# A router on rows before their normalisation, and a third down piece of 64 rows, in a one-core decoder layer

## The reference

```python
x = layernorm(x + attn(x, W_Q, W_K, W_V, W_O))                 # causal, 16 heads of 128
x = layernorm(x + xattn(x, ctx, Wq, Wg, bg, Wkv, Wo))          # linear cross attention with a gate, 375 keys
logits = x @ router_weight.T + router_bias                     # 8 experts
top_vals, top_idx = top_k(logits, 2); top_w = softmax(top_vals)
gate, up = split(x @ gate_up_proj[e] + gate_up_bias[e])        # H = I = 512
act = (clip(up, -7, 7) + 1) * min(gate, 7) * sigmoid(1.702 * min(gate, 7))
expert_out = act @ down_proj[e] + down_bias[e]
x = layernorm(x + sum over the two chosen experts of top_w * expert_out)
```

## Time and profile before

| | |
|---|---|
| median of 3 runs | 853.14 us (853.09 to 853.36) |
| the profiled execution | 854.54 us, of which 852.7 us are its span |
| TensorE busy | 832.9 us, 98% of the span, 4919 products |
| VectorE, ScalarE, GpSimd busy | 479.0, 319.1 and 97.3 us |
| read and written in memory | 64.10 and 31.53 MB |
| cross attention's last product to the first expert's first | about 625 to 649.9 us |
| the eight experts | 649.9 to about 836 us |

### The profile page before, as it was taken

How to read it: one execution, slowest core, us unless ns; L and a number is a source line. 1 busy time by engine, 2 the same in 40 slices (tenths; PEclk the granted TensorE clock), 3 DMA queues, 4 the chain that set the end, 5 groups by cost and what they waited for, 6 DMA issues and landing times.

```text
span 852.7 us, 12622 instructions
## 1 busy us (share of the span) xinstructions
PE 832.9 (98%) x4919; PEld 733.2 (86%) x4919; DVE 479.0 (56%) x878; ACT 319.1 (37%) x718; POOL 97.3 (11%) x92
## 2 busy tenths in 40 slices
PE   9999999999999999999999999999988999999995
PEld 7989898989899998988899888888867888888884
DVE  4536455363736462675760254455577687777765
ACT  4543324242433432442543222212233365555434
POOL 0000000000000000000000000110231244343432
PEclk9999999999999999999999999999976999999998
DMA  9990735533020003003110101110287366665235
GB/s 321 350 309 7 232 110 174 163 99 106 26 80 7 26 7 124 3 4 136 51 37 1 33 4 37 62 62 1 89 321 214 127 204 202 193 182 168 51 59 188
DMA packets 35759, 97.39 MB, mean 114 GB/s; under 512 B 6665, under 2 KB 9225, under 8 KB 33009
## 3 DMA queue, kind: packets, MB, share of 16 engines
q1 hardware_dynamic: 32224, 88.69, 30.8%
q0 software_dynamic: 3472, 7.87, 4.5%
HBM read 64.10 MB, written 31.53 MB: 112 GB/s over the span
## 4 chain that ended last, share of the span: by engine, by line
PE 93%; DVE 3%; ACT 2%; issue 1%; DMA 1%; POOL 0%; ACTq 0%; SPq 0%; POOLq 0%; DVEq 0%
PE bank L316 74%; PE bank L701 3%; PE bank L605 3%; PE bank L735 3%; PE bank L628 2%; PE bank L796 2%; PE bank L687 1%; PE bank L984 1%; PE bank L773 1%; PE bank L814 1%; ACT prob L1140 1%; PE bank L852 1%; DVE w_gu L1433 1%; DMA xg<-x_rows 0%; DMA x_rows<-row,slot_u 0%
## 5 line engine op out<-in xcount | busy, mean ns | idle before, releaser
L316 PE MATMUL bank<-w_kv,cT 128*125 128x512 f32 x576 | 143.6, 400 | 0.0
L316 PE MATMUL bank<-xT,w_qkv 128*128 128x512 f32 (+1 forms) x672 | 137.8, 365 | 0.8 <-ACT qT L1130 0.8
L316 PEld LDWEIGHTS bank<-xT,w_qkv 128*128 128x128 f32 x672 | 122.1, 188 | 15.8 <-ACT qT L1130 1.1
L316 PEld LDWEIGHTS bank<-w_kv,cT 128*125 128x125 f32 x576 | 104.2, 186 | 23.8
L316 PE MATMUL bank<-x_g,w_gu 128*128 128x288 f32 x768 | 111.2, 303 | 3.7 <-DVE x_g L1433 2.9
L316 PEld LDWEIGHTS bank<-x_g,w_gu 128*128 128x128 f32 x768 | 107.1, 194 | 5.3 <-issue 3.2
L501 POOL TENSOR_TENSOR ln_rs<-ln_ve,half 128x1 f32<-128x1 f32 (+2 forms) x16 | 11.3, 705 | 616.5 <-DVE ln_ve L1562 603.5
L316 PE MATMUL bank<-w_o,zT 128*128 128x512 f32 x336 | 78.7, 392 | 0.0
L316 PE MATMUL bank<-w_qkv,xT 128*128 128x256 f32 x588 | 77.3, 287 | 0.0
L316 PEld LDWEIGHTS bank<-w_o,zT 128*128 128x128 f32 x336 | 62.4, 188 | 12.7
L316 PEld LDWEIGHTS bank<-w_qkv,xT 128*128 128x128 f32 x588 | 72.2, 191 | 0.0
(11 more groups left out here) (174 smaller groups left out, 1202.5 us busy)
## 6 DMA issues: line engine op xcount, KB each, us to landing
x_rows<-blank SPq DMA_DIRECT2D x9, 2084.0 KB, 16.5
raw_gu<-in_w_gu_dram SPq DMA_DIRECT2D x8, 2048.0 KB
raw_w<-in_w_qkv_dram SPq DMA_DIRECT2D x22, 512.0 KB, 9.0
raw_dn<-in_w_down_dram SPq DMA_DIRECT2D x8, 1024.0 KB, 8.9
raw_c<-in_ctx_t_dram SPq DMA_DIRECT2D x8, 750.0 KB, 4.3
raw_o<-in_w_o_dram SPq DMA_DIRECT2D x8, 512.0 KB, 4.3
xg<-x_rows SPq DMA_DIRECT2D x8, 512.0 KB, 6.2
raw_kv<-in_w_kv_dram SPq DMA_DIRECT2D x2, 1024.0 KB, 6.8
```

The costliest lines, as they stand in the source:

```text
L316: last = nc.tensor.matmul(mm_out, lhs(a, k), rhs(b, k), start=(k == 0 and i == 0), stop=(k == n - 1 and i == 2))
```

## The change

1. **Router on the added rows.** `turn_x2` transposes `acc` after `cross_add`, not `row` after the normalisation. Since the logits are linear in the row, `choose` scales them by `ln_rs` and adds `rt_c`, which is the router's bias less mean x deviation x the column sums of the router's weights. `router_sums` makes these sums once, by four products behind the gates; `x2_norm` makes `shift` and `rt_c` for each tile. At the end the order is another: `turn_x2(5)` ahead of the last pass of `cross_out(6)`, `router(6)` ahead of `rank(5)`, `choose(5)` ahead of `x2_norm(6)`, on ScalarE a weight split between the two copies.
2. **First rows by part.** The first expert's rows are read in three transfers with a semaphore each, TensorE waits for each by itself, and SP issues nothing further until all three have landed.
3. **Third down piece.** For experts 0 to 5 the 32 high and the 32 low columns of `hT` lie side by side, and `down_stacked` takes both as one operand of 64 columns against the high weights, and the 32 high ones against the low weights: 8 products for 12. Rows 32 to 63 of the result are scaled as well and added to memory by a fourth adding transfer (`add_stacked`), which waits for the first three to land and stands behind `gated(e + 2, 0)` on GpSimd. `h_low` splits in two operations.
4. **Order in the first two experts.** High and low halves of the second expert's rows ahead of `swish` and `clamp`; the split of the first `w_dn` ahead of the loop on ScalarE and in two halves in parts 1 and 2 on VectorE; the weights of the third expert split a part earlier (`SPLITS`).

```diff
-            last = [("rk", 4), ("st", 0), ("t1", 5), ("rt", 5), ("t1", 6), ("rk", 5), ("rt", 6), ("db", 0), ("rk", 6),
+            last = [("rk", 4), ("st", 0), ("t1", 5), ("rt", 5), ("t1", 6), ("rt", 6), ("rk", 5), ("db", 0), ("rk", 6),
...
-        SPLITS = {0: ((3,), (), (), (), ()), 1: ((), (), (), (0,), (1, 2, 3))}
+        SPLITS = {0: ((3,), (), (), (), ()), 1: ((), (), (0,), (1,), (2, 3))}
...
-            for e in range(3):
+            for k, (p0, rows) in enumerate(PIECES):
+                sp.dma_start(xg[0][0:rows, k, :], x_rows_of(p0, rows)[:, 0:D]).then_inc(in_first[k], 16)
+            for k in range(3):
+                sp.wait_ge(in_first[k], 16)
+            for e in range(1, 3):
                 rows_in(xg[e], e * ROWS, in_xg[e])
...
+            def add_stacked(e):
+                p0, rows = PIECES[2]
+                pool.wait_ge(add_done, added_by(e) + 48)
+                nc.gpsimd.indirect_dma_start(
+                    y_acc, bass.IndirectOffsetOnAxis(ap=meta[0:rows, 2, e, NE:NE + 1].bitcast(U32), axis=0),
+                    y[rows:2 * rows, (3 * e + 2) % 4, :], None, bounds_check=T + DUMP - 1, oob_is_err=True,
+                    compute_op=ALU.add).then_inc(add_done, 16)
+
             for e in range(NE + 1):
                 if e < NE:
                     for q in range(KC):
                         gated(e, q)
+                        if q == 0 and 0 <= e - 2 < STACKED:
+                            add_stacked(e - 2)
...
             def turn_x2(n):
-                pe.wait_ge(m["row_ok"], n + 1)
+                pe.wait_ge(*done("wo", n))
...
-                    mm = nc.tensor.transpose(o[:, k * P:(k + 1) * P], row[:, n, k * P:(k + 1) * P], ident[:, :])
+                    mm = nc.tensor.transpose(o[:, k * P:(k + 1) * P], acc[:, n, k * P:(k + 1) * P], ident[:, :])
...
+            def router_sums():
+                pe.wait_ge(m["z_lo"], 4 * NP_)
+                pe.wait_ge(in_late, 16 * 2)
+                o = take(route, "ws", 0)
+                for k in range(KC):
+                    mm = nc.tensor.matmul(o[:, 0:NE], all_ones[:, :], rt_w[:, k, :], start=(k == 0), stop=(k == KC - 1))
+                mm.then_inc(ready("ws", 0)[0], 1)
...
-            cross_out(6)
+            cross_out(6, PASSES[0:2])
             turn_x2(5)
+            cross_out(6, PASSES[2:3])
             router(5)
             turn_x2(6)
+            router(6)
             rank(5)
-            router(6)
...
+            def down_stacked(w, hid, bk):
+                p0, rows = PIECES[2]
+                for b, i in ((0, 0), (1, 0), (1, 1), (0, 1), (1, 2), (0, 2), (1, 3), (0, 3)):
+                    wide = rows if b else 2 * rows
+                    mm = nc.tensor.matmul(banks[bk][0:wide, :], hid[:, i, p0:p0 + wide], w[:, b, i, :],
+                                          start=(b == 0 and i == 0), stop=(b == 0 and i == 3))
+                mm.then_inc(m["dn_mm"], 1)
...
             for k in range(3):
                 gather_high(0, k)
+            dn_high(0, 0)
...
-                    swish(e, q)
                     if e == 0 and q:
                         gather_high(1, q - 1)
+                    swish(e, q)
...
             def x2_norm(n):
                 normalise(1, n, n + 3, row[:, n, 0:D], "row_ok")
+                s = n % 2
+                nc.vector.tensor_tensor(shift[:, s:s + 1], ln_mv[:, 1, n, 0:1], ln_rs[:, 1, n:n + 1], ALU.mult)\
+                    .then_inc(m["rtc_ok"], 1)
...
+                nc.vector.scalar_tensor_tensor(rt_c[:, s], rt_s[:, :], shift[:, s:s + 1], rt_b[:, :], ALU.mult, ALU.add)\
+                    .then_inc(m["rtc_ok"], 1)
...
+                nc.vector.scalar_tensor_tensor(logit[:, s], bank("rt", n)[:, 0:NE], ln_rs[:, 1, n:n + 1], rt_c[:, s],
+                                               ALU.mult, ALU.add).then_inc(done("rt", n)[0], 1)
...
-                split_lo(hid[:, 1, q], hh[:, q % 2], hid[:, 0, q]).then_inc(m["h_lo"], 1)
+                for p0, rows in (PIECES[2], (0, 2 * P)):
+                    lo = split_lo(hid[:, q, hidden_cols(1, p0, rows)], hh[:, q % 2, p0:p0 + rows],
+                                  hid[:, q, p0:p0 + rows])
+                lo.then_inc(m["h_lo"], 1)
...
-                    clamp(e, q, gu_b[:, e])
                     if e == 0 and q:
                         gather_low(1, q - 1)
+                    if e == 0 and q in (1, 2):
+                        dn_low_half(0, 0, q - 1)
+                    clamp(e, q, gu_b[:, e])
```

More of the change, by code:

```diff
@@ L234, in decoder_layer @@
         in_xg = [sem(f"in_xg{j}") for j in range(3)]
+        in_first = [sem(f"in_first{k}") for k in range(3)]
         in_last = [sem(f"in_last{s}") for s in range(2)]
@@ L279, in route_order @@
         def route_order():
-            steps = []
+            steps = [("ws", 0)]
             for n in range(5):
@@ L336, in decoder_layer, with hidden_cols, added_by @@
         LAST_E = NE - 1
+        STACKED = NE - 2
+        def hidden_cols(a, p0, rows):
+            first = CAP + (p0 + CAP - 2 * P) % CAP if a else p0
+            return slice(first, first + rows)
+        def added_by(e):
+            return 48 * e + 16 * min(e, STACKED)
         HELD = (P, P, 2 * (CAP - 2 * P))
@@ L920, in _ @@
                 gate(j)
+            router_sums()
             for b, chunks in enumerate(CHUNKS):
@@ L1027, in down @@
                     pe.wait_ge(m["xg_lo"], 3 * (e + 2) + 2)
-                down_piece(w_dn[e % 2], hT[e % 2], k, y_bank(e, k))
+                if k == 2 and e < STACKED:
+                    down_stacked(w_dn[e % 2], hT[e % 2], y_bank(e, k))
+                else:
+                    down_piece(w_dn[e % 2], hT[e % 2], k, y_bank(e, k))
             for k in range(6):
@@ L1349, in y_evac @@
                 if i >= 4:
-                    act.wait_ge(add_done, 48 * ((i - 4) // 3 + 1))
-                rows = PIECES[k][1]
-                scaled(e, k, y_bank(e, k), i % 4, meta[0:rows, k, e, e:e + 1])
+                    held = (i - 4) // 3
+                    act.wait_ge(add_done, added_by(held + 1) if i % 3 == 0 else added_by(held) + 48)
+                rows = PIECES[k][1] * (2 if k == 2 and e < STACKED else 1)
+                scaled(e, k, y_bank(e, k), i % 4, meta[0:rows, k, e, e:e + 1], rows)
             def gather_high(e, k):
@@ L1380, in _ @@
                     y_evac(e - 1, 1)
-                if more:
+                if e and more:
                     dn_high(e, e % 2)
@@ L1701, in dn_low, with dn_low_half @@
                 split_lo(w_dn[s][:, 1], raw_dn[s], w_dn[s][:, 0]).then_inc(m["dn_lo"], 1)
+            def dn_low_half(e, s, h):
+                if h == 0:
+                    dve.wait_ge(m["dn_hi"], e + 1)
+                part = slice(h * KC // 2, (h + 1) * KC // 2)
+                last = split_lo(w_dn[s][:, 1, part], raw_dn[s][:, part], w_dn[s][:, 0, part])
+                if h:
+                    last.then_inc(m["dn_lo"], 1)
             nc.vector.memset(idle, 1.0).then_inc(m["gate_ok"], 1)
@@ L1816, in _ @@
             split_lo(dn_b[1][0:NE, :], raw_dnb[0:NE, :], dn_b[0][0:NE, :]).then_inc(m["dnb_lo"], 1)
+            dve.wait_ge(*ready("ws", 0))
+            nc.vector.tensor_scalar(rt_s[:, :], bank("ws", 0)[:, 0:NE], -1.0, None, ALU.mult).then_inc(done("ws", 0)[0], 1)
             for b, chunks in enumerate(CHUNKS):
@@ L1870, in _ @@
             cross_stats(6)
+            choose(5)
             x2_norm(6)
-            choose(5)
             assign(5)
```

48 lines of the change are left out of this document (28 added, 20 removed).

## The result

The changed kernel takes 844.88 us (median of 4 runs, 844.43 to 846.58) against 853.25 us of the kernel before on the same chip (853.09 to 854.08). The ratio is 0.9897, 95% interval 0.9884 to 0.991: 8.4 us less, where 10.8 were forecast (842.3 us, from 839.3 to 847.8). It lies in that range and 0.4 above the narrower one, 840 to 844.5, that the main forecast had. The spans of the profiled executions, 852.7 and 843.2, differ by 9.5.

A forecast was written before the change was run, and what follows sets the result against it. TensorE, busy 98% of the span, bounds the kernel. Terms 1.0 + 0.1 - 2.1 - 1.3 - 3.0 + 0 - 5.5 = -10.8 take the profiled 854.54 to 843.7, as median 842.3 us, range 839.3 to 847.8.

The forecast's parts named there:

- Column sums: `router_sums` puts four products of 8 columns into a dense TensorE stretch: cost +1.0 us, and +0.1 at most for `x2_norm`.
- Router end: Tiles transposed before normalisation, so the last slots and the scatter behind them come earlier: -2.1 us, bounds -1.4 and -2.6.
- First rows: First expert's rows read in parts, so pieces overlap and its first product starts earlier: -1.3 us, bounds -0.5 and -1.9.
- First to second expert: Hole of 1.77 us before the second expert's product shrinks to 0.35, clock stays full: -3.0 us, bounds 0 and -3.4.
- the 1.6 that I tied to the hole: After the idle 1.77 us, 48 products take 8.14 us at lowered clock against 6.56 at 2.4 GHz: 1.6 us.
- Second to third: Before the third expert a hole of 0.9 us stays, the third piece's 0.9 is kept: nothing more, bounds -0.8 and +0.5.
- Third down piece: Eight products of 0.23 us instead of twelve save 0.92 us in each of six experts: -5.5 us.
- The second add: `add_stacked` waits on GpSimd for the third add, landing taken as 3.5 us; `gated(e, 1)` done by 10.8: no cost.
- the prediction's own sign of being wrong: GpSimd's `pr` at part 1 later than 11 us into an expert, with TensorE waiting for `x_g` or `w_gu`.
- The rival of mildly late adds: Add landing of 5 to 6.7 us leaves holes up to 1.8 us in six experts: 843 to 853 us, chance 0.08.
- the drains: Third down piece: six extra width changes cost 0.16 us each, so it gains nothing: 847.8 us, chance 0.07.

The follow-up runs named there:

- experiments 7 and 8: Changed kernel with second add at part 2, two splits in part 2 (841.45 us): 7, first rows in two transfers, 843.45; 8, TensorE awaiting all three, 843.04.
- Experiment 10: Changed kernel with the order of splits and copies of the first two experts as before the change: 850.14 us, ratio 0.9951.
- experiment 3: Changed kernel with no expert stacked (`STACKED = 0`), third down piece of twelve products as before: 847.73 us, ratio 0.992.
- experiment 1: Changed kernel with the second add issued two products later on GpSimd, part 2 instead of part 0: 842.97 us, ratio 0.9862.
- experiment 2: Changed kernel with the low half of the `w_dn` split moved behind the next expert's part 0 clamp: 846.8 us, ratio 0.9905.

## Why the prediction was right, and where it was off

**Column sums.** Right: +1.04 in the traces before and after, 1.1 to 1.2 over all traces with and without them.

**Router end.** Right in mechanism. `choose(6)` starts at 631.67, which less the 1.04 is 630.63; the layout had it at 630.7. Then the last steps took longer than laid out. The timelines of TensorE, VectorE and GpSimd:

```profile
633.05 0.59 PE L860 MATMUL bank<-chosen,before 128*128 128x8 f32 x2 [1.21 <-DVE chosen L1717]
```

```profile
634.97 0.17 DVE L1744 CAST slot_u<-slot_f 128x2 uint32<-128x2 f32 x1
```

```profile
635.95 0.97 POOL L528 DMA_INDIRECT x_rows<-row,slot_u  x1 [1.03 <-DVE slot_u L1744]
```

The slots are out at 634.1 on the old scale instead of 633.3 to 633.8. The layout gave 2.6 to 3.1 us to the steps from `choose(6)` to the slots. The earlier trace rows have 3.32 for them (632.36 to 635.68), and after they took 3.47: `rank` and the count ran at 1.2 GHz both times (0.59 us, and 0.60 before, for what took 0.39 with tile 5). So the row was there and the term was laid out too short. GpSimd begins 0.81 behind the slots as laid out. -1.6 instead of -2.1.

**First rows.** Right: -1.8 for -1.3, within the bounds of -0.5 to -1.9. The first piece landed with 2.9 us about where the store of 256 KB had put it (3.0), and experiments 7 and 8 show both halves of it.

**First to second expert.** The hole was to shrink to 0.35 and went altogether, and the granted clock stayed at full: -3.85 for -3.0, of which 0.35 is part 0 (5.82 and 5.47), which varies from run to run. Experiment 10 shows that the 1.4 to 1.8 of the hole are the order's. It speaks against the 1.6 that I tied to the hole: with the same hole the clock did not fall. The 1.6 came in the traces all the same; as far as experiment 10 tells, that is luck. What the clock fell for in the kernel before stays open.

**Second to third.** The number is near the forecast (-0.71 for -0.9), and a hole stayed (1.06 for 0.9). But it is the earlier weight splits that bring it: without any stacking the stretch is as short (9.15, experiment 3).

**Third down piece.** Right in itself. The eight products step by 0.23 us where nothing holds them (752.19 less 750.35 is 1.84 for eight, in experiment 1), with 64, 32, 32, 64, 32, 64, 32 and 64 columns. There is no drain: a period of 21.57 is 22.57 less 1.0. Experiment 3 less experiment 1 gave 4.8 of the 5.5; five of the six pieces pay, the first does not. The rule weighed against it, from the Trainium skill, "TensorEngine Tiling (Array Packing)", section Tiling Modes, would make these six changes of width drain if they were changes of mode; no run here shows a drain.

**The second add** is the step that failed. The forecast had it at no cost: third add issued by 4.4 us into the expert, 3.5 to land, new issue over by 9.8, `gated(e, 1)` by 10.8. In the fifth expert it was issued by 7.5, the wait ended at 11.8 and `hidden(e, 1)`, which needs `gated(e, 1)`, began at 14.0. `gated(e, 1)` itself began 12.7 us into the expert, and TensorE then waited for `x_g`, which is the prediction's own sign of being wrong. The rival of mildly late adds (843 to 853, chance 0.08) is what happened. Its price of 2.2 us in these traces is more than the 1.3 by which the sum was missed; the other terms together came out 0.9 better than forecast. The term failed in two places. The larger is the issue, 3.1 us later than the 4.4 allowed for: I took the adds' start from the steady state before and did not ask what the wait itself does to the next expert's start (2.4), nor what `w_dn`'s split does to an issue that falls behind its start (2.0; the third issue and the pauses were 0.4 shorter, and 0.9 was in the forecast). The smaller is the landing: the wait for it ended 3.0 to 4.5 us behind the end of the issue, 4.3 in the fifth expert, for 3.5; I took it from a quiet stretch plus a little. The two hang together, for in experiment 2 the issue was early and the landing took 7.0.

The terms add to 1.04 - 1.58 - 1.77 - 3.85 - 0.71 - 2.46 - 0.2 = -9.5 of span against the sum of -10.8. That the medians differ by 8.4 and not by 9.5 comes from the profiled executions: before's lies 1.3 above its median, after's (845.05) 0.2. So of the 2.6 us by which 842.3 was missed, 1.3 are terms, and nearly all the rest is that I carried the 1.4 between profile and median of the kernel before over to the changed one.

The range owes something to luck. Its upper end, 847.8, is the price of the drains, which did not come. Its lower end does not follow from what it names: 0.5, 0.6 and 0.4 better for router, reads and hole give 840.8, not 839.3.

## What to carry to other kernels

A wait for a transfer's landing that is put into an in-order queue is paid by everything behind it, so give it a place where nothing that matters is queued behind it; two products later made 2.2 us free here. When its landing time is unknown, look at what is in flight in the same microseconds: the same add took 3.6 to 7.5 us to land here, the most beside reads of rows. When a start waits for a read, cut the read at the unit of the first work and begin on the first part (1.4 us here), and lay out each converting step by when its consumer needs it, not by where it belongs (3.2 us here up to the third expert).

## What the runs showed of the hardware

- An add's issue on GpSimd takes 1.56 us and took 3.56 when VectorE had begun its 2.29 us split of `w_dn` 0.17 us earlier (732.51 and 732.68); it took 2.42 where the split had begun 1.31 us earlier (731.54 and 732.85, experiment 1), and 1.56 where the split began 0.26 us after it (738.36 and 738.62 in the kernel before) or lay elsewhere (experiment 2). In these rows who begins first decides, and an issue that falls into the split ends 1.2 to 1.4 us behind the split's end. The Trainium skill, "SBUF — State Buffer", section "Who interferes with whom", tells of an exclusive lock on a port pair that both engines share, which goes to whoever issues first; that agrees. It also says that an operation of two inputs, as this split is, contends with GpSimd's reads, but that it was not seen to stall a transfer; here one did, by 2.0 us.
- The third add of 32 rows landed 3.6 to 5.2 us after the start of its issue in the kernel after, and 7.5 in experiment 2, where it was issued 2.2 us earlier in the expert; the fourth add, with the DMA engines idle, 3.0 to 3.1.
- One transfer of 512 KB and one of 64 KB had all landed 4.48 us after the first issue, with other reads behind them; the same rows in 256, 256 and 64 KB, with no reads behind them, 3.94.
- The same hole of 1.77 us was followed by a granted clock of 0.51 in one kernel and of 1.00 in another (experiment 10).
- The same kernel's TensorE came back from 1.2 to 2.4 GHz some 3 us apart behind the start of the first expert in its two profiles, which makes 1.4 us of the time.
